# ScalarE for one PSUM copy, statistics at other ticks, and output products two by two in one bank

## The reference

```python
xn = layernorm(x)
q  = (xn @ Wq.T + bq) * 16**-0.5          # 16 heads of 16
kv = xn @ Wkv.T + bkv                     # one k, one v for all heads
att = softmax(q_heads @ k.T) @ v          # 16*512 rows x 512 keys, per batch
a  = att @ Wo.T + bo
tokens = einsum(A, B)                     # 6 experts x 100 tokens
attn   = softmax(xn @ tokens.T / 16)      # per expert
delta  = (((attn[1:] @ val[1:]) + xn) @ wd.T + wd_b) * scale
f  = log(sum(exp(delta) * gates))         # gates: top-1 softmax
out = x + a + (xn + f)
```

## Time and profile before

| | us |
|---|---|
| median of 3 runs | 896.31 (896.04 to 896.63) |
| the profiled execution | 896.53 |
| its span | 894.7 |
| granted clock of TensorE, mean | 0.977 |

### The profile page before, as it was taken

One profiled execution on the slowest core, in us unless ns is written; L12 is line 12 of the kernel. 1 busy time (PEld: TensorE's weight loads), 2 busy tenths in 40 slices (PEclk: granted clock), 3 DMA queues, 4 the chain that ended last, 5 costly groups with the idle time before them and its releaser, 6 DMA issues. The chain is left out here.

```text
span 894.7 us, 18186 instructions
## 1 busy us (share of the span) xinstructions
PE 837.3 (94%) x6038; PEld 274.5 (31%) x6038; DVE 780.8 (87%) x1504; ACT 676.4 (76%) x1371; POOL 568.4 (64%) x754
## 2 busy tenths in 40 slices
PE   5679999999999999999999999999999999999987
PEld 4233223332323333332323233232333323232213
DVE  8698897989989898998989899898989899898926
ACT  2227887887888888787888878788887888888884
POOL 2875677584867768485776848477784858646321
PEclk9688999999999999999999999999999999999989
DMA  4422243635334444534434353443435344141112
GB/s 118 116 60 48 81 88 86 129 98 124 92 106 86 115 103 108 119 86 117 87 101 111 99 119 86 119 99 93 103 105 119 86 127 109 60 102 63 61 50 73
DMA packets 125076, 86.09 MB, mean 96 GB/s; under 512 B 57143, under 2 KB 109112, under 8 KB 124984
## 3 DMA queue, kind: packets, MB, share of 16 engines
q1 hardware_dynamic: 124504, 84.56, 38.5%
q10 hardware_dynamic: 480, 0.36, 0.1%
HBM read 39.30 MB, written 33.54 MB: 81 GB/s over the span
## 5 line engine op out<-in xcount | busy, mean ns | idle before, releaser
L857 DVE TENSOR_REDUCE M<-pA 128x1 f32<-128x512 f32 x1024 | 649.0, 682 | 73.6 <-PE pA L358 69.8
L656 ACT ACTIVATE P<-pB 128x512 f32<-128x512 f32 x1002 | 554.1, 603 | 132.9 <-PE pB L363 128.2
L358 PE MATMUL pA<-K,Q 48*128 48x512 f16 x1024 | 322.4, 387 | 28.8 <-DVE M L857 13.2
L363 PE MATMUL pB<-Q,K 50*128 50x512 f16 x1002 | 315.5, 385 | 0.3 <-DVE M L857 0.2
L376 PE MATMUL pO<-P,VK 128*32 128x512 f32 x2048 | 273.9, 607 | 4.1 <-ACT P L656 3.5
L358 PEld LDWEIGHTS pA<-K,Q 48*128 48x128 f16 x1024 | 67.7, 94 | 341.7 <-DVE M L857 289.5
L376 PEld LDWEIGHTS pO<-P,VK 128*32 128x32 f32 x2048 | 40.5, 108 | 99.9 <-issue 55.0
L1005 POOL TENSOR_SCALAR Cz<-Cx 128x512 f32<-128x512 f32 x32 | 62.1, 1940 | 13.4 <-ACT Cx L638 13.4
L363 PEld LDWEIGHTS pB<-Q,K 50*128 50x128 f16 x1002 | 64.0, 94 | 8.2 <-ACT P L656 5.9
L1012 POOL TENSOR_TENSOR Rs<-Rs,Cz 128x512 f32<-128x512 f32 x32 | 40.7, 1271 | 35.6 <-ACT Cz L644 33.5
L970 POOL CAST Qp<-qf 128x512 f16<-128x512 f32 x31 | 18.9, 608 | 63.7 <-ACT qf L605 63.6
(11 more groups left out here) (172 smaller groups left out, 868.7 us busy)
## 6 DMA issues: line engine op xcount, KB each, us to landing
o_parts<-OTr SPq DMA_DIRECT2D x62, 256.0 KB, 2.2
X<-in_x SPq DMA_DIRECT2D x16, 512.0 KB, 3.9
q_pieces<-Qp SPq DMA_DIRECT2D x64, 128.0 KB
out<-OUT SPq DMA_DIRECT2D x32, 256.0 KB, 3.8
Op<-o_parts SPq DMA_DIRECT2D x31, 256.0 KB
Rb<-l_parts SPq DMA_DIRECT2D x31, 256.0 KB
Q<-q_pieces SPq DMA_DIRECT2D x30, 256.0 KB, 4.5
Q<-q_pieces SPq DMA_DIRECT2D x34, 128.0 KB, 4.6
```

What stands on the lines that cost most here:

```text
L358: e.matmul(bank1("ab", t)[:, :], Q16[r:r + 48, b % 3, h, 128 * s:128 * s + 128], K16[r:r + 48, b % 3, :], start=True, stop=True).then_inc( ...
L363: e.matmul(bankB(t)[:, :], K16[r:r + 50, b % 3, 128 * i:128 * i + 128], Q16[r:r + 50, b % 3, :, 32 * hh:32 * hh + 32], start=True, stop=Tr ...
L656: e.activation(P[:, u % PR, :], bankB(u + LB)[:, :], ACT.Exp, scale=alpha).then_inc(S("e"))
L857: e.tensor_reduce(M[:, t // 32 % 2, t % 2, t % 32 // 2:t % 32 // 2 + 1], bank1("ab", t)[:, :], AX, ALU.max, negate=True).then_inc(S("mx"))
```

## The change

- The o products of all batches but the last: o0 and o1 are made one after the other, six matmuls each, into the two halves of one pA bank at tick 31, o2 and o3 at tick 55 (before: ticks 7, 31, 35 and 55, each with its own turn). One DVE instruction of 512 columns adds the residual for both (before two of 256).
- UK is copied by ACT for every batch, at the same slot.
- d1 with its exponential moves from tick 3 to tick 7, the guard of the first half from 6 to 9, its logarithm from before the exponential of tick 12 to after q0's copy at the same tick.
- The four bn_stats go from ticks 31 to 34 to 22.6, 24, 25.6 and 27, the aggregate from 35 to 28.2; var, root, refine, norm, the split (ph, pl), the residual, the load and the splits of q and k get other slots.
- One memset is dropped at the start (the column is written by a reduction anyway), and POOL's `on` gets one more wait, on its own earlier step.

```diff
 SLOT = {
...
-    "load": -116, "stats0": -97, "stats1": -96, "stats2": -95, "stats3": -94, "aggr": -93, "var": -92.4,
-    "root": -91.4, "refine": -90.2, "norm": -83.4, "ph": -78.2, "pl": -76.9, "xtd": -66.2,
-    "residual": 10.2, "q0": -53, "qe0": -51.4, "qs0": -46.5, "qw0": -44, "uk": -49, "uke": -47.4, "ks": -44.2,
-    "kd": -41.6, "vg": -45, "vge": -44.3, "q1": -41, "qe1": -39.4, "qs1": -38.2, "qw1": -35.6,
+    "load": -112.2, "stats0": -105.4, "stats1": -104, "stats2": -102.4, "stats3": -101, "aggr": -99.8, "var": -99,
+    "root": -98.2, "refine": -97.2, "norm": -93.6, "ph": -83.4, "pl": -78.9, "xtd": -66.2,
+    "residual": 12.9, "q0": -53, "qe0": -51.4, "qs0": -43.8, "qw0": -41.4, "uk": -49, "uke": -47.4, "ks": -41.5,
...
-    "d0": -1, "dexp0": -0.4, "d1": 3, "dexp1": 3.6, "guard0": 6.1, "dlog0": 12.2, "radd0": 15.9,
+    "d0": -1, "dexp0": -0.4, "d1": 7, "dexp1": 7.6, "guard0": 8.8, "dlog0": 13.2, "radd0": 18.5,
...
-    "o0": 135, "fo0": 135.6, "o1": 159, "fo1": 159.6, "st0": 163.2, "o2": 163, "fo2": 163.6, "o3": 183,
-    "fo3": 183.6, "st1": 188.6,
+    "o0": 159, "fo0": 159.6, "st0": 163.2, "o2": 183,
+    "fo2": 183.6, "st1": 188.6,
 }
...
 LAST = {
-    "o0": 113.2, "o1": 115.4, "o2": 115.8, "o3": 116.3, "fo0": 126, "fo1": 126.1, "st0": 127, "fo2": 127.8,
-    "fo3": 128.8, "st1": 129,
+    "o0": 113.2, "o2": 115.8, "fo0": 126, "st0": 127, "fo2": 127.8, "st1": 129,
 }
-LAST_BUT_ONE = {"o3": 171, "fo3": 171.6, "st1": 172.2}
+LAST_BUT_ONE = {"o2": 171, "fo2": 171.6, "st1": 172.2}
...
 TAIL = {
+    "o1": 115.4, "o3": 116.3, "fo1": 126.1, "fo3": 128.8,
...
-            "o0": lambda b: (S("fo"), 4 * b + 1), "o1": lambda b: (S("fo"), 4 * b + 2),
-            "o2": lambda b: (S("fo"), 4 * b + 3), "o3": lambda b: (S("fo"), 4 * b + 4),
+            "o0": lambda b: (S("fo"), 4 * b + (2 if b < NB - 1 else 1)), "o1": lambda b: (S("fo"), 4 * b + 2),
+            "o2": lambda b: (S("fo"), 4 * b + (4 if b < NB - 1 else 3)), "o3": lambda b: (S("fo"), 4 * b + 4),
...
-            return (bank2 if (t, b) == (3, NB - 1) else bank1)(f"o{t}", b)[:, 0:C]
+            if b < NB - 1:
+                return bank1(f"o{t - t % 2}", b)[:, C * (t % 2):C * (t % 2) + C]
+            return (bank2 if t == 3 else bank1)(f"o{t}", b)[:, 0:C]
...
-                        for part in range(parts):
-                            for k, (wp, op) in enumerate(PIECES):
-                                mm = e.matmul(bankO(t, b), OnP[:, b % 2, part, op, 128 * t:128 * t + 128],
-                                              woP[:, wp, part, :], start=(part == 0 and k == 0), stop=(part == 1 and k == 2))
-                        if parts == 2:
-                            mm.then_inc(S("o"))
+                        for u in (t, t + 1) if parts == 2 else (t,):
+                            for part in range(parts):
+                                for k, (wp, op) in enumerate(PIECES):
+                                    mm = e.matmul(bankO(u, b), OnP[:, b % 2, part, op, 128 * u:128 * u + 128],
+                                                  woP[:, wp, part, :], start=(part == 0 and k == 0),
+                                                  stop=(part == 1 and k == 2))
+                            if parts == 2:
+                                mm.then_inc(S("o"))
...
-                if due("uke", n) == 0:
-                    w.wait_ge(S("uk"), 1)
+                if (b := due("uke", n)) is not None:
+                    w.wait_ge(S("uk"), b + 1)
                     w.wait_ge(S("bks"), 3)
-                    e.activation(UK[0:UKW, :], bank1("uk", 0)[0:UKW, :], ACT.Identity, scale=uks[0:UKW, 0:1],
+                    w.wait_ge(S("utm"), b)
+                    w.wait_ge(S("kl"), b)
+                    e.activation(UK[0:UKW, :], bank1("uk", b)[0:UKW, :], ACT.Identity, scale=uks[0:UKW, 0:1],
                                  bias=ukb[0:UKW, 0:1]).then_inc(S("uke"))
...
-                    e.memset(bmx[:, 3:4], 0.0).then_inc(S("wm"))
...
-                if (b := due("uke", n)):
-                    w.wait_ge(S("uk"), b + 1)
-                    w.wait_ge(S("bks"), 3)
-                    w.wait_ge(S("utm"), b)
-                    w.wait_ge(S("kl"), b)
-                    e.tensor_scalar(UK[0:UKW, :], bank1("uk", b)[0:UKW, :], uks[0:UKW, 0:1], ukb[0:UKW, 0:1],
-                                    ALU.mult, ALU.add).then_inc(S("uke"))
-
...
                 for t in range(4):
                     if (b := due(f"fo{t}", n)) is not None:
-                        w.wait_ge(S("o"), 4 * b + t + 1)
                         w.wait_ge(S("r2"), 2 * b + t // 2 + 1)
                         w.wait_ge(S(f"st_{t // 2}"), 16 * b)
-                        e.scalar_tensor_tensor(out=OUT[:, t, :], in0=bankO(t, b), scalar=scl[:, 9:10],
-                                               in1=Rs[:, b % 5, t, :], op0=ALU.mult, op1=ALU.add).then_inc(S("fo"))
+                        if b < NB - 1:
+                            w.wait_ge(S("o"), 4 * b + t + 2)
+                            e.scalar_tensor_tensor(out=OUT[:, t:t + 2, :].rearrange("p i c -> p (i c)"), in0=bank1(f"o{t}", b)[:, :],
+                                                   scalar=scl[:, 9:10], in1=Rs[:, b % 5, t:t + 2, :].rearrange("p i c -> p (i c)"),
+                                                   op0=ALU.mult, op1=ALU.add).then_inc(S("fo"), 2)
+                        else:
+                            w.wait_ge(S("o"), 4 * b + t + 1)
+                            e.scalar_tensor_tensor(out=OUT[:, t, :], in0=bankO(t, b), scalar=scl[:, 9:10],
+                                                   in1=Rs[:, b % 5, t, :], op0=ALU.mult, op1=ALU.add).then_inc(S("fo"))
...
+                    w.wait_ge(S("onl"), nh)
```

More of the change, by code:

```diff
@@ L38 @@
 SLOT = {
-    "load": -116, "stats0": -97, "stats1": -96, "stats2": -95, "stats3": -94, "aggr": -93, "var": -92.4,
-    "root": -91.4, "refine": -90.2, "norm": -83.4, "ph": -78.2, "pl": -76.9, "xtd": -66.2,
-    "residual": 10.2, "q0": -53, "qe0": -51.4, "qs0": -46.5, "qw0": -44, "uk": -49, "uke": -47.4, "ks": -44.2,
-    "kd": -41.6, "vg": -45, "vge": -44.3, "q1": -41, "qe1": -39.4, "qs1": -38.2, "qw1": -35.6,
+    "load": -112.2, "stats0": -105.4, "stats1": -104, "stats2": -102.4, "stats3": -101, "aggr": -99.8, "var": -99,
+    "root": -98.2, "refine": -97.2, "norm": -93.6, "ph": -83.4, "pl": -78.9, "xtd": -66.2,
+    "residual": 12.9, "q0": -53, "qe0": -51.4, "qs0": -43.8, "qw0": -41.4, "uk": -49, "uke": -47.4, "ks": -41.5,
+    "kd": -38.8, "vg": -45, "vge": -44.3, "q1": -41, "qe1": -39.4, "qs1": -37, "qw1": -34.4,
     "vt": -37, "vte": -36.4, "gate": -34.8, "mask": -32.6, "mkd": -31.4,
@@ L89 @@
 DVE_NAMES = ("rngq", "rng", "two", "scl", "wl", "scd", "stats0", "stats1", "stats2", "stats3", "aggr", "refine", "xl0", "xl1",
-             "uke", "qs0", "gate", "smax", "ssum", "mm", "mx", "rec", "fo0", "fo1", "fo2",
+             "qs0", "gate", "smax", "ssum", "mm", "mx", "rec", "fo0", "fo1", "fo2",
              "fo3", "nl00", "nl01", "nl02", "nl03", "nl10", "nl11", "nl12", "nl13")
@@ L704, in _ @@
                                     apply_absolute_value=True).then_inc(S("wm"))
-                    w.wait_ge(S("wm"), 10)
+                    w.wait_ge(S("wm"), 9)
                     e.scalar_tensor_tensor(out=wmx[:, 2:3], in0=amx[:, 0:1], scalar=amx[:, 1:2], in1=wmx[:, 0:1],
                                            op0=ALU.max, op1=ALU.max).then_inc(S("wm"))
-                    w.wait_ge(S("wm"), 11)
+                    w.wait_ge(S("wm"), 10)
                     e.scalar_tensor_tensor(out=rng[:, :], in0=wmx[:, :], scalar=float(C), in1=bmx[:, :],
```

## The result

The changed kernel takes 905.06 us (median), the kernel before beside it 896.17: 8.9 us more, ratio 1.0095, 95% interval 1.0079 to 1.011. Profiled a second time beside another set of the kernel before, it stood at 1.0084 (1.0064 to 1.0104). Slower, as forecast, and inside the range; but by 7.3 to 8.9 us where the sum gave 4.0.

What follows compares the result with a forecast made beforehand. PE was taken as the bound, with DVE counting only where PE waits for it. Full periods at +0.50 us gave 11 x 0.50 = +5.5; with the other periods, start and end +4.0: 896.3 + 4.0 = 900.3 us, range 895.5 to 907.

Steps and rivals of the forecast that it cites:

- mt alone, d1, o2: Ticks 3 and 35, where mt loses d1 and o2 beside it: new PE wait of 0.76 us each, +1.52 a period.
- DVE's lateness gone: PE's waits at o2 and tick 36 for DVE after its statistics, 0.81 us a period, go and don't reappear earlier.
- My walk of DVE's queue: Starts of DVE's reductions stepped through from tick 22 to 32: only tick 33 waits, by 0.09 us.
- Joins: Ticks 31 and 55: fewer tile switches, -0.24 us a period; wider addition costs 0, bounds 0 and 0.44 twice a period.
- ACT's log and copy: Ticks 12 to 19: moved logarithm and UK copy on ACT, +0.18 us a period; bounds 0 to 0.67 + 0.5.
- The -0.7 that I took from DVE: Period 0, set by DVE around tick 18, loses one UK copy: -0.7 us, bounds -0.8 and +0.5.
- Mask, refine, norm and utm keep 2 us or more: After POOL's moved steps and the later load of X, these steps still have 2 us of room; no cost.
- POOL or the load is late: Rival: X late for statistic 0, or mt's maxima late; 0.5 us a period, 12 periods, +6, 906 us; chance 0.10.
- The 0.97 saved on the earlier trace: Period 2: the first o product's wait of some 0.97 us for its input's split goes; period -0.5 us.
- Period 15: Last period, with neither statistics nor UK copy: 1.52 - 0.24 - 0.24 = +1.0 us.
- The end: PE's wait near 859 us for last batch but one's o0 goes: -3.2 us, +0.3 for the wider addition.
- The rivals of the other sign: Faster: PE's waits after mt are DVE's and vanish with the statistics, about 878 us, 890 with half; chance 0.12.

Runs made afterwards that it cites:

- a1_fill: The changed kernel with the transposition mt issued eight times over into the same place; 906.3 us (ratio 1.0124).
- b1: The kernel before with the change's slots for all steps from stats0 to pl, and one setup memset left out; 893.25 us (ratio 0.9961).
- c1: The kernel before with DVE's statistics at the change's slots (not batch 0), last batch but one's o0 24 ticks later, the wait before On; 888.06 us, repeated 887.93.
- a5: The changed kernel with the copy of UK by DVE again, nothing else; 905.9 us (ratio 1.0104).
- a4: The changed kernel with d1, its exponential, guard and logarithm back at the slots of before; 897.56 us (ratio 1.0017).
- a8: The changed kernel with var, root, refine, norm, ph and pl at the slots of before; 902.8 us (ratio 1.0064).
- a3: The changed kernel with the guard of the first batch's mask at slot 28.9 instead of 30.8; 904.4 us (ratio 1.0100).
- a7: The kernel before with only the change's joined products and double additions, and the change's end; 898.56 us (ratio 1.0016).

## Why the prediction was right in its periods and short in its sum

First and second pair of profiles, against the forecast (us; period 15 and end run from the first score product of period 15 to the end of the span):

| part | forecast | first | second |
|---|---|---|---|
| start and period 0 | -0.6 | +2.65 | -0.84 |
| period 1 | +0.3 | +1.03 | +1.47 |
| period 2 | -0.5 | -0.47 | +0.51 |
| periods 3 to 13 | +5.5 | +5.89 | +6.17 |
| period 14 | +1.2 | +1.27 | +1.30 |
| period 15 and end | -1.9 | -1.63 | -1.77 |
| sum | +4.0 | +8.7 | +6.8 |

- **mt alone, d1, o2: right.** 0.76 twice a period, and a1_fill shows that it is a wait.
- **DVE's lateness gone and "not born again earlier": right here, and only here.** It holds since the pair at tick 31 fills the time in which DVE is late. In the kernel of before the same move brings back 0.4 of 0.81 (b1, c1). My walk of DVE's queue was made for the changed kernel, and its result may not be carried to another.
- **Joins: right**, 1.41 from start to start, the bank in time. The addition takes 746 ns; I took 803 from a row of another operation, between bounds of 476 and 952.
- **ACT's log and copy: right in sum** (+0.22 against +0.18, ticks 16 and 18), but its split depends on the order: taken out alone, the copy gives back 0.02 (a5) and the logarithm with d1 0.12 (a4), and the copy left behind then costs 0.10.
- **Period 0: the failed step, in its first part.** The sum put POOL's moved steps and the later load of X at nothing, with "Mask, refine, norm and utm keep 2 us or more"; that was read in steady periods. The -0.7 that I took from DVE is there (double ticks 18 and 20). But in period 0 POOL's queue has no such room:

```profile
57.22 0.23 POOL L904 TENSOR_SCALAR ve<-mv 128x4 f32<-128x4 f32 x1 [1.62 <-DVE mv L788]
...
59.01 0.20 POOL L914 TENSOR_TENSOR rstd<-y 128x4 f32<-128x4 f32 x1
59.17 1.94 POOL L1008 TENSOR_SCALAR Cz<-Cx 128x512 f32<-128x512 f32 x1
...
62.88 0.30 POOL L993 TENSOR_SCALAR Ms<-M 128x32 f32<-128x32 f32 x1
```

```profile
63.84 0.31 PE L509 MATMUL pB<-idh,M 128*64 128x128 f16 x1 [2.71 <-POOL M L997]
```

```profile
60.89 0.31 PE L507 MATMUL pB<-idh,M 128*64 128x128 f16 x1 [1.46 <-POOL M L994]
```

  These are POOL and PE of after, and PE of before. Variance and refinement run ahead of the guard, so mt starts at 63.84 instead of 60.89. Double ticks 24 to 38 together take 14.91 instead of 13.94, +0.97, in both pairs of profiles. POOL's steps are 1.3 of that: with them back, a8 takes 13.62. The other 0.3, with the opposite sign, is DVE's moved statistics, which I had not priced in period 0. What is left of the first comparison's 2.65 is the scatter of the first 88 us told above.
- **The late transposed mask: the failed step, in its second part.** The room for utm went in the DMA queue. I had foreseen that the load of X would slide by 2.8 us, and it does (issued 9.7 us after the start of period 8 in the kernel before, 12.5 in the changed one), but I had not walked what stands behind it in SyncE's in-order queue. SP and POOL of period 8, first of the changed kernel (the period starts at 453.02), then of a4_d1_back (449.20):

```profile
465.47 0.40 SPq L1066 DMA_DIRECT2D X<-in_x  x1
...
480.45 1.72 SPq L1080 DMA_TRANSPOSE mkT<-mk  x1
...
484.71 1.16 POOL L988 TENSOR_TENSOR UTm<-UK,mkT 96x512 f32<-96x512 f32 x1 [0.24 <-DMA mkT<-mk]
```

```profile
459.02 0.40 SPq L1066 DMA_DIRECT2D X<-in_x  x1
...
475.44 1.28 SPq L1080 DMA_TRANSPOSE mkT<-mk  x1
...
480.27 1.15 POOL L988 TENSOR_TENSOR UTm<-UK,mkT 96x512 f32<-96x512 f32 x1
```

  The write of the results, the exchange of the sums, q's pieces and then the transposition of the mask all follow the load in that queue. With d1 at tick 3 the mask lands at a median of 29.3 to 30.2 us after the period's start, and at 32.2 at the latest (thirteen kernels or repeats); with d1 at tick 7 the median is 31.8 to 32.2, and the latest 33.1 to 34.6 (seven). In all twenty, over periods 1 to 14, a period whose mask lands by 33.5 has no wait, and each of the twelve in which it lands after 33.7 has one, of 0.1 to 1.4 us at tick 43:

```profile
225.66 1.15 POOL L988 TENSOR_TENSOR UTm<-UK,mkT 96x512 f32<-96x512 f32 x1 [2.75 <-DMA mkT<-mk]
```

  So some 2 us of the room are gone in every period, 1.3 are left in the median, and the scatter of the transfer itself (3.9 to 6.0 us from issue to landing in the changed kernel) decides in which ones PE sees it. That is why the waits change periods from one execution to the next, why a8, with POOL's order back, kept them, and why a3, whose latest mask lands at 33.1, shows none: its edit moves one step of the first batch and nothing in this queue, so there it was luck. a4 takes all of them away; a run that moves the load alone was not made. I gave "POOL or the load is late" 0.10, as a cost of every period.
- **Period 2: a reading of one execution.** The 0.97 saved on the earlier trace rows was a wait that the second profile of before has not: without it the period is +0.5, 1.0 more than forecast. The wait is of a kind that comes now and then: seven of the nine kernels or repeats with a product at tick 7 and d1 at tick 3 have it in one or two of periods 2 to 13, at 0.15 to 0.96 us, and the four without that product never. So moving o0 away does save such a wait, but a rare one, and not 0.97 in period 2 of every execution.
- **Period 15: 0.45 more** (up to its last score product, +1.46 and +1.45 instead of +1.0). The logarithm waits for the guard, which came later with d1, and exponentials stand behind it:

```profile
828.69 0.63 ACT L650 ACTIVATE Cz<-Cx 128x512 f32<-128x512 f32 x1 [0.42 <-POOL Cx L1010]
```

  I had walked this only in a steady period, where the guard is in time.
- **The end: right**, -3.09 and -3.22 (forecast -2.9).

Together: 4.0 + 1.0 (period 0, ticks 24 to 38) + 1.1 to 1.7 (mask, the two profiles of after) + 0.1 (the rest of period 1) + 1.0 (period 2) + 0.45 (period 15) - 0.2 to 0.3 (end) = 7.5 to 8.0, between the 7.3 and 8.9 of the two comparisons. The steady periods, which are most of the sum, came out. The rivals of the other sign fell with a1: the wait's label said DVE, and DVE was done.

By single edits, a steady period of 51.72 changes by -0.39 (statistics alone), +0.28 (joins alone), +0.36 (d1 with guard and logarithm, taken out of the changed kernel) and +0.02 (copy of UK). These do not add up to +0.49, since statistics and joins share a tick (the spread is worth 0.28, not 0.39, once the pair stands at tick 31) and the copy of UK and the logarithm share another. Taken in one order, through kernels that were run, they do: 51.72, with the joins 52.00 (a7), with the statistics and the copy 51.84 (a4), with d1, guard and logarithm 52.20.

## What to carry to other kernels

A product is cheap where the engine waits for something else anyway, and how cheap is the wait less the work that fills it: read that for each place from starts, not from busy time or the wait's label. When a step moves, walk every in-order queue that it touches (also those of engines that only make a round trip, and that of the DMA issues), and walk it in the first and last periods too, where the slack of the steady ones is not there. A wait that one profile shows in one period alone is not a term of a sum before a second profile shows it.

## What the runs showed of the hardware

- Executions of one kernel differ by 1.4 us (before) and 2.1 us (after) in the first 88 us, and the mean granted clock of one and the same 6 us of nearly full work by up to 0.24; periods at full clock repeat to 0.02 us, but for single waits.
- A two-tensor operation of DVE out of PSUM costs 476 ns for 256 columns and 746 for 512, so two joined save 0.21 us; one tensor and two scalars took 803 at that width. The group in the changed kernel, 240 to 766 us:

```profile
L879 DVE SCALAR_TENSOR_TENSOR OUT<-pA,scl,Rs 128x512 f32<-128x512 f32 x20 | 14.9, 746 | 4.5 <-PE pA L521 4.5
```

- Two products of 256 columns into the two halves of one PSUM bank run without a gap: 1.41 us from start to start, where twice a single one is 1.54. The difference, 0.13, is my estimate of one change between tile shapes: no run isolates it.
- A small transposing transfer took 3.9 to 6.0 us from issue to landing in the periods of one execution (the mask, changed kernel).
